# A hybrid of two attentions and an expert layer on one core: one running list of row maxima, with new borders between pairs of heads

## The reference

```python
x = x + L0_conv_ref(gn(x))      # attention 0: qkv with bias, relative positions, softmax over all 1024 keys
t = t + L1_attn_ref(ln(t))      # attention 1: causal softmax
t = t + L1_ffn_ref(ln(t))       # 4 experts with GELU, top 2 by gate
```

## Time and profile before

| | us |
|---|---|
| median of 3 runs | 2025.42 (2024.59 to 2038.48) |
| the profiled execution | 2029.26 |
| its span in the profile | 2027.5 |
| PE busy | 1737.5 (86%) |
| PEld busy | 710.0 (35%) |
| DVE busy | 1223.0 (60%) |
| ACT busy | 1065.5 (53%) |
| POOL busy | 297.7 (15%) |

### The profile page before, as it was taken

One profiled execution on the slowest core, in us unless ns is written; L12 is line 12 of the kernel. 1 busy time (PEld: TensorE's weight loads), 2 busy tenths in 40 slices (PEclk: granted clock), 3 DMA queues, 4 the chain that ended last, 5 costly groups with the idle time before them and its releaser, 6 DMA issues.

```text
span 2027.5 us, 26496 instructions
## 1 busy us (share of the span) xinstructions
PE 1737.5 (86%) x9900; PEld 710.0 (35%) x9900; DVE 1223.0 (60%) x2498; ACT 1065.5 (53%) x1377; POOL 297.7 (15%) x191
## 2 busy tenths in 40 slices
PE   1578488998899988998899988998889989998858
PEld 0123233343333433343333433343333433334333
DVE  6753577556764677646775577736775466744631
ACT  1245435574456734674456734666456745555433
POOL 6102101401032100501023010501014010200000
PEclk7589579999999999999999999999999999999979
DMA  6645454445535345445345246354434455323000
GB/s 174 140 88 155 109 139 81 104 113 172 94 65 155 104 122 104 103 117 156 75 89 154 74 141 112 81 153 128 96 77 104 113 164 92 72 43 93 14 11 8
DMA packets 63751, 212.23 MB, mean 105 GB/s; under 512 B 17415, under 2 KB 19080, under 8 KB 51207
## 3 DMA queue, kind: packets, MB, share of 16 engines
q1 hardware_dynamic: 61702, 210.04, 41.9%
q10 hardware_dynamic: 1920, 0.49, 0.1%
HBM read 115.62 MB, written 81.79 MB: 97 GB/s over the span
## 4 chain that ended last, share of the span: by engine, by line
PE 61%; DVE 19%; ACT 7%; DMA 6%; issue 4%; SPq 3%; POOL 0%; ACTq 0%; DVEq 0%
PE psOM L777 15%; PE psS L716 14%; DVE mx L1466 8%; PE psT L746 7%; PE psT L893 5%; PE psS L907 5%; PE psT L749 4%; DVE mrow L1568 3%; PE psT L666 2%; DVE qs L1595 2%; DVE x L1577 1%; ACT probs L1147 1%; DMA qs<-scr_h 1%; DMA qr<-negb 1%; DMA qs<-negr 1%
## 5 line engine op out<-in xcount | busy, mean ns | idle before, releaser
L1147 ACT ACTIVATE probs<-psT 128x1024 f32<-128x1024 f32 (+7 forms) x768 | 617.8, 836 | 494.3 <-PE psT L746 239.3
L1466 DVE TENSOR_REDUCE mx<-psS 128x1 f32<-128x512 f32 (+3 forms) x1152 | 687.0, 641 | 284.6 <-PE psS L716 231.3
L777 PE MATMUL psOM<-probs,v 128*32 128x256 f32 (+2 forms) x3948 | 396.3, 439 | 17.8 <-ACT probs L1147 16.5
L746 PE MATMUL psT<-qs,ks 128*128 128x512 f32 x768 | 328.0, 510 | 35.1 <-DMA qs<-negr 15.6
L716 PE MATMUL psS<-ka,qa 128*128 128x512 bf16 x768 | 308.6, 403 | 37.8 <-DVE mx L1466 22.1
L749 PE MATMUL psT<-qr,kr 97*128 97x512 bf16 (+3 forms) x576 | 184.9, 350 | 4.7 <-DMA qr<-negb 3.7
L893 PE MATMUL psT<-xf,w1s 97*128 97x512 f32 x384 | 183.4, 610 | 2.1 <-DVE mrow L1568 1.8
L716 PEld LDWEIGHTS psS<-ka,qa 128*128 128x128 bf16 x768 | 74.4, 97 | 314.6 <-DVE mx L1466 225.1
L907 PE MATMUL psS<-probs,w2s 128*96 128x512 f32 x384 | 181.9, 599 | 0.8 <-ACT att L1206 0.8
L1595 DVE TENSOR_TENSOR qs<-psOM,qs 32x768 fp32r<-32x768 f32 x128 | 121.8, 952 | 95.7 <-ACT qs L1181 93.7
L746 PEld LDWEIGHTS psT<-qs,ks 128*128 128x128 f32 x768 | 140.9, 198 | 110.2 <-ACT probs L1147 42.6
(11 more groups left out here) (163 smaller groups left out, 1650.3 us busy)
## 6 DMA issues: line engine op xcount, KB each, us to landing
qs<-scr_w SPq DMA_DIRECT2D x48, 512.0 KB, 5.3
qs<-scr_q SPq DMA_DIRECT2D x48, 384.0 KB, 7.5
scr_q<-split SPq DMA_DIRECT2D x32, 384.0 KB, 4.2
scr_k<-split SPq DMA_DIRECT2D x32, 384.0 KB, 4.7
scr_w<-qs SPq DMA_DIRECT2D x8, 1536.0 KB, 13.1
scr_h<-qs SPq DMA_DIRECT2D x16, 768.0 KB, 14.9
qs<-scr_h SPq DMA_DIRECT2D x96, 128.0 KB, 5.3
qr<-scr_q SPq DMA_DIRECT2D x8, 1152.0 KB, 7.7
```

The costliest lines, as they stand in the source:

```text
L746: last = mm(o[:, a:b], ks[:, p % 2, hh, keys], qs[:, p % 2, kt // 2 % 2, hh, a:b], start=True, stop=True)
L777: last = mm(psO[j:j + 2 * HD, i * P:b * P], v[:, kt, p, hh * HD:(hh + 2) * HD], x, start=kt == 0, stop=kt == (NT - NC + c if layer else NT ...
L1147: A(probs[:, n % 4, q0:T], psT[:, t_slot(ts, m), q0:T], ACT.Exp).then_inc(t_free, 1)
L1466: V.reduce_max(mx[layer][:, p % 2, (h % 2) * NT + t, kc:kc + 1], psS[:, s_bank(st, fill), 0:max_cols(layer, t, kc)], AX).then_inc(s_free, 1)
```

## The change

The fills of an attention and of those that follow it become one list (`stream`), from which each pair takes two pieces: `ahead`, spread over the points of steps 0 to 5 as before, and `tail`, which belongs to the pair after the next one and is issued in steps 6 and 7, one fill at each point in layer 0 (8 fills) and at each second point in layer 1 (6 fills). What is left of the tail is issued after the last `values`. The cut of `values` into lots stays as it is.

| pair | fills in steps 0 to 5, before | now | in steps 6, 7, now |
|---|---|---|---|
| attention 1, p = 0 | 18 | 18 | 6 |
| attention 1, p = 1 | 24 own + 8 lead | 18 own | 6 lead |
| attention 1, p = 2 | 24 lead | 26 lead | 6 of attention 0 |
| attention 0, p = 0 | 32 | 26 | 8 |
| attention 0, p = 1 | 32 | 24 | 0 |
| attention 0, p = 2 | 0 | 0 | 0 |

The first attention 0, which has no attention 1 before it, has 32 and 8 in pair 0. Attention 1 of the last item has 18 and 6, then 18, then none. On VectorE `group_var` moves from 6 to 12 reductions behind `group_stats`, and `group_norm` from 22 to 24, behind `mrow` of the pair. The number of instructions of each kind is the same.

```diff
--- before.py
+++ after.py
@@ -70,7 +70,20 @@
 
 MAX_STEPS = {"attn0": max_steps(0, range(2, NH)), "attn1": max_steps(1, range(2, NH)), "lead": max_steps(0, range(2))}
 PER_PAIR = [len(MAX_STEPS[s]) // (PAIRS - 1) for s in ("attn0", "attn1")]
-LEAD_EARLY = 8
+TAIL = {0: 8, 1: 6}
+
+
+def stream(layer, p, lead, first):
+
+    later = [("attn0", f) for f in range(2 * PER_PAIR[0])]
+    if layer:
+        own = [("attn1", f) for f in range(2 * PER_PAIR[1])]
+        later = own + [("lead", f) for f in range(len(MAX_STEPS["lead"]))] + later if lead else own
+    ends = [0, PER_PAIR[1], 2 * PER_PAIR[1], 2 * PER_PAIR[1] + len(MAX_STEPS["lead"])] if layer else [0, PER_PAIR[0], 2 * PER_PAIR[0], 2 * PER_PAIR[0]]
+    begin = ends[p] + TAIL[layer] if p else LEAD if layer else 0 if first else TAIL[1]
+    return later[begin:ends[p + 1]], later[ends[p + 1]:ends[p + 1] + TAIL[layer]]
+
+
 MAXES = [("max", i) for i in range(2 * NT)]
 
 
@@ -751,7 +764,7 @@
                                     last = mm(o[:, a:a + P], ident_b[:, :], mask_k[:, :], start=False, stop=True)
                         if c == NC - 1:
                             last.then_inc(t_full, 1)
-                        between()
+                        between(kt)
 
                 def values(p, kt, between=None):
 
@@ -779,9 +792,8 @@
                             if lot == len(lots) - 1:
                                 last.then_inc(p_used, 1)
                         if lot < len(lots) - 1:
-                            between()
-
-                n = PER_PAIR[layer]
+                            between(kt + 1)
+
                 lead = layer == 1 and next_lead(it)
                 if layer == 1:
                     pe.wait_ge(l1_in, upto("l1_in", it, "attn1", 0))
@@ -790,23 +802,26 @@
                 for p in range(PAIRS):
 
                     next_q = layer == 0 and p == 1 and next_layer0(it)
-                    skip = LEAD if layer == 1 and p == 0 else 0
-                    ahead = [(st, f) for f in range(p * n + skip, (p + 1) * n)] if p + 1 < PAIRS else []
-                    if lead and p:
-                        early = range(LEAD_EARLY) if p == 1 else range(LEAD_EARLY, len(MAX_STEPS["lead"]))
-                        ahead += [("lead", f) for f in early]
-                    points, sent = [0], [0]
-
-                    def between():
-
-                        points[0] += 1
-                        until = min(len(ahead), len(ahead) * points[0] // (6 * (NT - 2) - 2 - layer))
-                        for stage, fill in ahead[sent[0]:until]:
+                    ahead, tail = stream(layer, p, next_lead(it), it is None)
+                    points, sent = [0], [0, 0]
+
+                    def issue(fills):
+
+                        for stage, fill in fills:
                             if stage == "lead" and fill == 0:
                                 pe.wait_ge(ab_in, upto("ab_in", it, "lead", 0))
                                 pe.wait_ge(rel_lead_bf, upto("rel_lead_bf", it, "lead", 0))
                             max_scores(it, stage, fill)
-                        sent[0] = until
+
+                    def between(kt):
+
+                        points[0] += 1
+                        until = min(len(ahead), len(ahead) * points[0] // (6 * (NT - 2) - 2 - layer))
+                        issue(ahead[sent[0]:until])
+                        sent[0] = max(sent[0], until)
+                        if kt >= NT - 2 and sent[0] == len(ahead) and points[0] % (1 + layer) == 0:
+                            issue(tail[sent[1]:sent[1] + 1])
+                            sent[1] += 1
 
                     pe.wait_ge(negmax_in, upto("negmax_in", it, st, 16 * p))
                     if layer == 0:
@@ -835,6 +850,7 @@
                             elif kt == NT - 2:
                                 tr_norm(it)
                     values(p, NT - 1)
+                    issue(tail[sent[1]:])
 
             def res_norm(it):
 
@@ -1627,11 +1643,10 @@
                 maxima(it, "attn1", range(per))
                 if next_layer0(it):
                     group_stats(it, "gn")
-                    maxima(it, "attn1", range(per, per + 6))
+                    maxima(it, "attn1", range(per, per + 12))
                     group_var(it, "gn")
-                    maxima(it, "attn1", range(per + 6, per + 22))
+                    maxima(it, "attn1", range(per + 12, 2 * per))
                     group_norm(it, "gn")
-                    maxima(it, "attn1", range(per + 22, 2 * per))
                 else:
                     maxima(it, "attn1", range(per, 2 * per))
                 if next_lead(it):
```

## The result

The changed kernel takes 2007.08 us (median of seven, 2000.28 to 2013.43) where the kernel before took 2025.38 beside it (seven, 2022.52 to 2038.48): a ratio of 0.9907 [0.9879, 0.9935]. That is 18 us faster, where 38 were forecast, and lies at the bound of 1% that a measurement of this kernel can tell from no change: the interval reaches to both sides of it. The profiled execution took 2013.43, its span is 2011.6; before it was 2027.5.

A forecast was written before the change was run, and what follows sets the result against it. VectorE's reductions, 0.60 us each, were taken to pace the fills where these come every 0.46 us on TensorE. Terms summed to -37.6 us from 2029.3, giving 1991.7 profiled and a median of 1988, range 1968 to 2008.

The forecast's parts named there:

- The first step: Attention 0: fills 0.60 to 0.71 us apart wait for VectorE's reductions, against 0.46 when nothing holds them.
- Rival B: Fill distances of 0.60 to 0.71 are TensorE's own, so spreading gains nothing: 2045 us, chance 0.05.
- Its price: Attention 0, pair 1: 24 fills almost without waits instead of 32, -4.2 us a pair (bounds -2.6 and -4.8), -33.6 in eight.
- That sign: Attention 0, pair 1: hardly any weight load of a fill waits for a reduction.
- my part on the rest: Mix, projections, pair 2 of attention 0: no fills moved; DMAs and GpSimd's work are issued relative to the pairs and move along.
- Attention 0, pair 0: 26 fills save 3.4 us, the tail adds 2.3 to 2.5: net -1.1, -7.7 in seven items; first item +2.0.
- Attention 1, pair 0: Third tail fill waits behind `group_stats`, delaying the transposition: +2.4 us in six items (+14.4), +0.6 in two (+1.2).
- Attention 1, pairs 1 and 2: Pair 1, fewer fills: -4.0 in six items (-24), -5.8 in the last two; pair 2, more fills: +1.7 each, +11.9.
- The clock: TensorE's clock falls at half of 12 new stops in attention 1, +5.4; tail fills give back 1 to 2: net +4.
- A: Rival: attention 1's pair borders cost twice as much, clock low at all 20 borders: 2008 to 2018 us, chance 0.14.
- C: Rival: no clock fall at new stops or attention 0's start, few waits in its pair 0: 1975 us, chance 0.15.
- the forecast's own sum: All parts together -37.6 us from the profiled 2029.3, giving 1991.7, and a median of 1988; chance 0.66.

The follow-up runs named there:

- attention 0 alone: Kernel before with the new fill borders in attention 0 only (32 + 8 and 24 fills), attention 1 as before: 2017.64 us, ratio 0.9943.
- the late tail: Changed kernel with attention 1's tail fills starting one step later, in step 7, behind the transposition: 1993.68 us, ratio 0.9837.
- the two with both repairs: Changed kernel, `mrow` by one reduction and attention 1's tail behind the transposition: 1983.57 us, 0.9776; same with four tail fills there instead of six: 1976.72 us, 0.9749.
- the group edit: Changed kernel with `group_stats` behind the six tail reductions and `group_norm` behind the first six of lead on VectorE: 1994.24 us, ratio 0.9827.
- the earlier order: Changed kernel with `group_var` and `group_norm` back at 6 and 22 reductions behind `group_stats`: 2010.75 us, ratio 0.9923.
- both first edits: Changed kernel with `mrow` by one reduction, `group_stats` behind the tail reductions and `group_norm` behind the first six of lead: 1991.82 us, ratio 0.9814.

## Why the prediction was half right

**The first step held.** Distances of 0.60 to 0.71 us between fills were a wait for VectorE. Pair 1 of attention 0 was to be at 27.8 and 24.5, and came to 28.5 and 25.9, while 30 would have refuted it. Rival B, by which nothing is gained there, falls.

**Its price was too high.** It was -4.2 a pair, and -3.47 came with projections: 0.43 for each of the eight fills left out. I took the upper end, in which almost no wait is left (24 fills at 0.24), and wrote that hardly any weight load would wait for a reduction there. That sign didn't come. Waits of weight loads in the window of one such pair, before and then after:

```profile
PEld psS L716 <- DVE mx L1466: 9.1, 22, 0.8
```

```profile
PEld psS L729 <- DVE mx L1482: 4.9, 13, 0.8
```

Thirteen of 22 are left, and the 4.2 us of waiting that went are of the size of the 3.47 that the pair gained. In the pair without projections something else was uncovered, the one new wait. Waits in its window, us in total, times, longest, and TensorE at that place:

```profile
PE psT L759 <- DMA qs<-scr_h: 1.2, 1, 1.2
```

```profile
1762.54 0.39 PE L729 MATMUL psS<-ka,qa 128*128 128x512 bf16 x1
1764.12 0.50 PE L759 MATMUL psT<-qs,ks 128*128 128x512 f32 x1 [1.19 <-DMA qs<-scr_h]
```

The load of the next query operand is issued by SP at 1759.58, behind eight gathers that it had from 1754.60 on. In the kernel before it is issued as long after the pair's start (8.2 us) but wanted 2 us later, so the longer pair hid it; the words "move with them" in my part on the rest were wrong for this one. It doesn't always show: in four other kernels with the same fills in this pair and the load issued at the same place (attention 0 alone, the late tail, and the two with both repairs) nothing waits for it for long and the pair takes 24.6 to 25.0 us, close to the 24.5 of the forecast. Both together are 6.7 of the 21.7 us missed.

**Attention 0, pair 0: the step that failed.** "Net -1.1" counted fills and waits for their reductions. With `mrow` out of GpSimd's way the pair gives -0.9, so the net was right, but luck has a part in it: the six fills fewer are worth 2.5 to 2.8 and not 3.4, the eight tail fills cost 1.6 to 2.0 and not 2.3 to 2.5, and the two errors cancel. What the sum lacked was the neighbour: VectorE's one instruction with two SBUF inputs in that place, 0.01 us away from GpSimd's end before the change. I asked of the transposition what stands ahead of it in TensorE's queue, and never asked of `mrow` what runs beside it on GpSimd. The row is 10.4 of the 21.7 us, and in three of seven items the stop was followed by a fall of the clock. That doesn't belong to the stop: in the three kernels that keep the long `mrow` with its tail fills (the group edit, the earlier order, the late tail) it is as long in all 21 places, and no low clock follows it in any. The stretch around such a fall in the changed kernel, columns as above:

```profile
590.50:593.90 3.40, 3.40 (x13) 0.89 (x13) 1.42 (x3) 0.94 (x2) 0.00 (x0) 0.51 0.00 0
```

**Attention 1, pair 0: right.** +2.4 in six items was forecast, by a transposition 3.9 us after the last fill, and 2.38 from there to the next scores. TensorE and then VectorE there:

```profile
287.67 0.39 PE L729 MATMUL psS<-kr,qr 96*128 96x512 bf16 x1
...
291.23 0.34 PE L729 MATMUL psS<-kr,qr 96*128 96x384 bf16 x1 [1.17 <-DVE mx L1482]
...
291.46 0.27 PE L740 MATMUL psOM<-cst,mrow 128*16 128x128 f32 x1
...
293.83 0.39 PE L762 MATMUL psT<-qr,kr 97*128 97x512 bf16 x1
```

```profile
288.99 1.28 DVE L1442 BATCH_NORM_STATS2 gs<-xg 96x6 f32<-96x512 f32 x2
...
290.89 0.61 DVE L1482 TENSOR_REDUCE mx<-psS 128x1 f32<-128x128 f32 x2
```

287.67 to 291.46 is 3.79 us, and 291.46 to 293.83 is 2.37. The third fill waits for the reduction that `group_stats` holds up. The earlier trace rows gave this to 0.1 us. The 2.38 from the transposition to the scores doesn't hold everywhere, though: it is 3.2 to 3.3 us in three of the six items here, and 2.6 to 3.8 at four of the ends of pair 1. There TensorE stands up to 1.35 us for the DMA `qr<-negb`: the scores start 2.0 to 3.2 us after its issue, where it is 1.8 elsewhere. The forecast had it as fixed, and no run shows what makes it late. Over eight items the row is +16.9 against +15.6.

**Attention 1, pairs 1 and 2: right.** -30.9 against -29.8, and +2.07 each against +1.7. The gap behind the transposition of pair 2 is as long as before (2.8 us), so these 0.4 lie ahead of it.

**The clock: right in size by luck, wrong in place.** Of the 12 new stops in attention 1 one was followed by a low clock (the window from 755.80, 0.81, 23.6 us instead of 20.1), where I had taken six. It fell instead behind the `mrow` stop in three of seven items, 1.5 us each, and it no longer falls at the start of attention 0, which gives 4.4 us where I had taken 1 to 2. Together 3.5 + 4.5 - 4.4 is 3.6 us, and the forecast had 4. The rule of the Trainium skill that the prediction weighed (page "TensorE: Matmul & The Clock Gate", section on psum-queue depth-cycling), read as the prediction read it, would have had all 12, and the trace bears it out at that one. The page itself tells of one kernel in which the clock swings as TensorE idles briefly between its groups, and doesn't say that every stop does it.

**Of the rivals,** A gave 2008 to 2018 and so nearly the time, but not by its mechanism: it had the clock low at 20 borders, and it was low at one. Of C one part came true, the clock that stays up at the start of attention 0. Nor did the forecast's own sum decide alone: 2007 is that sum with a stall that no rival had (10.4 with its row), a price in pair 1 of attention 0 that was too high (6.7), and some 6 us of start, mix and ends. That the time lies inside the range, 1 us from its end, is luck in part: the end was worked out from other causes.

## What to carry to other kernels

Before shortening a stretch, list for each small instruction on the path of the latency-critical chain what runs beside it on the other engines at that moment: one that misses a neighbour by 0.01 us may hit it as soon as the change moves it. Work issued in exact order just ahead of a transposition or of the first product of a pair costs the time by which that work's own consumer is late, and the same work just behind costs little as long as it fits into the gap (here four fills of 0.60 us in 2.4 to 2.8 us cost 0 to 0.5 us, six cost 1.1 to 1.7); so size the tail by the gap, not by what is left to spread. A PE that is 97% busy can still give 3.5 us in 32, if the distances between its starts are those of another engine's instructions.

## What the runs showed of the hardware that was not expected

- A VectorE instruction of 128x32 with two SBUF inputs stretches from 0.19 us to 1.43 (after), and to 1.90 beside a GpSimd product of 1.89, and ends with GpSimd's. The same result by a reduction with one SBUF input takes 0.22 us beside the same GpSimd work.
- A stop of TensorE alone doesn't decide whether its granted clock falls. Behind one and the same stop of 1.44 us the granted clock fell to 0.50 in three of 28 places, all three in one kernel. At the start of attention 0 it was low in 10 of 21 places in the three kernels without tail fills at the end of attention 1, and in none of 70 in the ten with them; what of that is the fills' doing was not taken apart.
- The same instructions (a mix with pair 2 of attention 0) take 104.7 us at a mean granted clock of 0.99 and 107.8 at 0.96 (time at 0.50, which is 1.2 GHz, against 1.00, 2.4 GHz). This varies within one and the same kernel. In the kernel with `mrow` by a reduction and the late tail, the six such stretches were 104.9, 106.5, 107.5, 104.9, 105.4 and 108.8 us, with 0.9, 6.4, 9.3, 2.4, 2.7 and 9.6 us at clock 0.50. In the kernel with both first edits it fell at the same place in five items of six. I know of no way to tell from the profile of before where it will fall. What decides it stays open; all that the runs show is that edits in the pairs, which leave this stretch as it is, go with a shift of it, of up to 15 us in a kernel of 2000, and that an edit's own gain is to be read in its own windows.
